# A decoder layer on one core: the mixing product in quarters of the array, and the attention's output product from rounded parts

## The reference

```python
x = x + mamba(layernorm(x), W_in, conv_w, ..., W_out)
x = x + cross_attention(layernorm(x), ctx, mask, Wq, ..., Wo, qn_w, kn_w)
x = x + bitlinear_ffn(layernorm(x), w_gate, w_up, w_down, ln_weight)
```

## Time and profile before

| | |
|---|---|
| time, median of 3 runs | 1300.21 us (1299.61 to 1300.24) |
| the profiled execution's own time | 1300.34 us |
| its span, first to last instruction | 1298.4 us |
| busy share of the span | PE 95%, weight loads 79%, DVE 79%, POOL 61%, ACT 54% |
| chain that ended last | PE 87%, DVE 5%, POOL 3% |
| mean granted clock of TensorE | 0.978 |

### The profile page before, as it was taken

How to read it: one execution, slowest core, us unless ns; L and a number is a source line. 1 busy time by engine, 2 the same in 40 slices (tenths; PEclk the granted TensorE clock), 3 DMA queues, 4 the chain that set the end, 5 groups by cost and what they waited for, 6 DMA issues and landing times.

```text
span 1298.4 us, 32119 instructions
## 1 busy us (share of the span) xinstructions
PE 1229.9 (95%) x10803; PEld 1024.4 (79%) x10803; DVE 1031.4 (79%) x2572; ACT 703.5 (54%) x1588; POOL 796.1 (61%) x1435
## 2 busy tenths in 40 slices
PE   4789999999999999999999999999999999999865
PEld 3677888888888888888888888888888888888743
DVE  3675888888888888888888888888888888888555
ACT  3564566555555655555565555556555555665432
POOL 3465666667666666766666676666667666666541
PEclk8799999999999999999999999999999999999986
DMA  8300000000000000000000000000000000000000
GB/s 272 112 13 13 10 14 18 16 12 16 16 8 12 16 16 12 16 16 8 12 16 16 12 16 16 9 11 16 16 12 16 16 12 8 12 14 13 6 5 9
DMA packets 30645, 28.62 MB, mean 22 GB/s; under 512 B 7696, under 2 KB 28944, under 8 KB 30352
## 3 DMA queue, kind: packets, MB, share of 16 engines
q1 hardware_dynamic: 27680, 28.11, 6.8%
q10 hardware_dynamic: 2928, 0.03, 0.1%
HBM read 23.93 MB, written 4.19 MB: 22 GB/s over the span
## 4 chain that ended last, share of the span: by engine, by line
PE 87%; DVE 5%; POOL 3%; issue 2%; ACT 1%; DMA 1%; POOLq 0%; DVEq 0%; SPq 0%; ACTq 0%
PE bank L1405 17%; PE bank L1315 16%; PE bank L1397 5%; PE bank L1238 5%; PE bank L1375 4%; PE bank L1288 4%; PE bank L1247 4%; PE bank L1278 3%; PE bank L1425 3%; PE bank L1210 2%; PE bank L1430 2%; PE bank L1328 2%; PE bank L1227 2%; PE bank L1443 2%; PE bank L1385 2%
## 5 line engine op out<-in xcount | busy, mean ns | idle before, releaser
L1315 PE MATMUL bank<-xcT,wq 128*128 128x128 f32 x2048 | 236.2, 276 | 1.6 <-ACT xcT L648 1.6
L1315 PEld LDWEIGHTS bank<-xcT,wq 128*128 128x128 f32 x2048 | 231.1, 192 | 6.2 <-issue 2.0
L1405 PE MATMUL bank<-wo,oT 128*128 128x256 f32 x1024 | 232.1, 380 | 0.0
L1405 PEld LDWEIGHTS bank<-wo,oT 128*128 128x128 f32 x1024 | 190.6, 191 | 23.9 <-issue 0.3
L877 DVE SCALAR_TENSOR_TENSOR xc<-bank,cw,xc 128x124 f32<-128x124 f32 (+2 forms) x576 | 163.9, 341 | 15.2 <-ACT xc L618 8.4
L663 ACT ACTIVATE qT<-bank,bqT 128x128 f32<-128x128 f32 x384 | 109.7, 369 | 47.1 <-PE bank L1315 46.8
L354 POOL TENSOR_SCALAR m_mv<-m_mv 128x1 f32<-128x1 f32 x32 | 7.7, 241 | 158.1 <-DVE m_mv L845 158.1
L422 POOL TENSOR_TENSOR rq<-rq,minus_half 128x16 f32<-128x16 f32 x32 | 93.1, 2909 | 7.8 <-DVE rq L975 7.8
L1031 DVE SCALAR_TENSOR_TENSOR h<-h,bank 128x512 f32<-128x512 f32 x64 | 44.1, 688 | 64.9 <-ACT h L702 64.9
L434 POOL TENSOR_TENSOR pr<-pr,mask 128x512 f32<-128x512 f32 x64 | 82.9, 1315 | 14.0 <-DVE pr L982 14.0
L444 POOL TENSOR_TENSOR pr<-pr,mx 128x512 f32<-128x512 f32 x64 | 65.4, 1044 | 40.3 <-DVE mx L994 40.3
(11 more groups left out here) (225 smaller groups left out, 3053.7 us busy)
## 6 DMA issues: line engine op xcount, KB each, us to landing
x_in<-in_x SPq DMA_DIRECT2D x32, 128.0 KB, 2.1
c_in<-in_ctx SPq DMA_DIRECT2D x32, 128.0 KB, 2.0
x_m<-in_x SPq DMA_DIRECT2D x32, 128.0 KB, 2.0
out<-x SPq DMA_DIRECT2D x32, 128.0 KB, 1.7
wq<-in_L_xattn_Wq SPq DMA_DIRECT2D x1, 2048.0 KB, 14.3
wo<-in_L_xattn_Wo SPq DMA_DIRECT2D x1, 2048.0 KB, 12.7
w_in<-in_L_attn_W_in SPq DMA_DIRECT2D x1, 1024.0 KB, 6.0
qT<-in_L_ffn_w_gate SPq DMA_DIRECT2D x1, 1024.0 KB, 9.4
```

The source lines that it names most:

```text
L1315: last = mm(x_Qbank[g][:, (n % 4) * P:(n % 4 + 1) * P], wq[:, c, n * HD:(n + 1) * HD], xcT[:, c, :], start=(c == 0), stop=(c == DC - 1))
L1405: last = mm(X1[:, 0:D], oT[:, n, :, :], wo[:, n, :], start=(n == 0), stop=(n == NH - 1))
```

## The change

There are two parts.

The mixing product runs in quarters. `mbd` gives way to `mw`, which holds for each sequence only its own 64 x 64 block, so DVE writes it with one operation instead of two, and the clearing goes. PE multiplies with 64 rows, 64 weight columns and 64 moving columns, 16 times (32 instructions); the first sequence's results go to M0 and the second's to M2. As M2 is also where the squares are added up, `x_sums` now waits for `m_y` and not for `m_Xdt`. The product `x * D` goes to POOL (`m_skip`, into `xd`), and DVE's gate becomes two additions in place of four operations.

The output product becomes a `split_product`. `wo` is kept as `wo_hi` and `wo_lo`, `oT` as `o_hi` and `o_lo`; that makes 48 single-pass instructions with 256 moving columns. The rounded parts come from ACT (four copies, as before). The remainders of two banks come from DVE (`x_o_low`, out of PSUM) and of the other two from POOL, out of two more ACT copies (`x_o_copy`, into `o_f`, which lies in `ksq` and `th`). ACT now adds the keys' squares up itself, with four accumulating instructions, and `x_k_sum` goes. ACT's second tanh of the feed-forward part moves ahead of the keys' squares, and DVE's `m_norm` moves behind the second `x_o_low`. The output product also waits for the remainders from X1 and F1, the key and value products wait for those steps that read their banks, and `f_up` waits for the copy out of F1. At the start Wo is loaded in two halves through one staging area; the second half is loaded when POOL has finished the first (`w_o_low`).

```diff
             def x_output(t, half):
                 if half == 0:
-                    after(pe, x_oT[1][1], t + 1)
+                    after(pe, x_ol[1][1], t + 1)
+                    after(pe, x_ol[0][1], t + 1)
                 for n in range(half * NH // 2, (half + 1) * NH // 2):
-                    last = mm(X1[:, 0:D], oT[:, n, :, :], wo[:, n, :], start=(n == 0), stop=(n == NH - 1))
+                    last = split_product(X1[:, 0:D], (o_hi[:, n, :, :], o_lo[:, n, :, :]), (wo_hi[:, n, :], wo_lo[:, n, :]),
+                                         n == 0, n == NH - 1)
...
-                for n in range(NHM):
-                    last = mm(M0[(n % 2) * HP:(n % 2 + 1) * HP, (n // 2) * P:(n // 2 + 1) * P], xdt[:, n, :], mbd[:, n, :],
-                              start=True, stop=True)
+                for j in range(XCH):
+                    for a in range(2):
+                        rows = slice(a * SEQ, (a + 1) * SEQ)
+                        for u in range(2):
+                            last = mm(m_mixed[a][u * HP:(u + 1) * HP, j * SEQ:(j + 1) * SEQ], xdt[rows, 2 * j + u, :],
+                                      mw[rows, 2 * j + u, :], start=True, stop=True)
...
+            def m_skip(t):
+                after(pool, s["m_xs"], t + 1)
+                after(pool, s["m_y"], t)
+                g.tensor_tensor(xd[:], xc[:, 0:XCH, :], bcast(d_ch[:, :].unsqueeze(2), [P, XCH, P]),
+                                ALU.mult).then_inc(s["m_xd"].sem, 1)
...
+            def x_o_low(t, n):
+                after(pool, x_of[n], t + 1)
+                heads = slice(8 * n, 8 * n + 8)
+                g.tensor_tensor(o_lo[:, heads, n, :], o_f[n], o_hi[:, heads, n, :].bitcast(F32),
+                                ALU.subtract).then_inc(x_ol[n][n].sem, 1)
+
+            def w_o_low(n):
+                pool.wait_ge(s["p_ohi"].sem, n + 1)
+                heads = slice(8 * n, 8 * n + 8)
+                g.tensor_tensor(wo_lo[:, heads, :], wo_stage, wo_hi[:, heads, :].bitcast(F32),
+                                ALU.subtract).then_inc(s["p_olo"].sem, 1)
...
-            def x_k_square(t):
+            def x_k_square(t, xb):
                 after(act, s["x_kb"], t + 1)
-                sc.activation(ksq[:], kb[:], ACT.Square).then_inc(s["x_ksq"].sem, 1)
+                if xb is not None:
+                    after(act, x_ol[0][0], xb + 1)
+                for n in range(NKV):
+                    last = sc.activation(ksq[:, n, :], kb[:, n, :], ACT.Square, accum_out=kss[:, 0, n:n + 1])
+                last.then_inc(s["x_ksq"].sem, 1)
...
-                for j in range(XCH):
-                    last = v.scalar_tensor_tensor(out=yT[:, j, :], in0=xc[:, j, :], scalar=d_ch[:, j:j + 1],
-                                                  in1=M0[:, j * P:(j + 1) * P], op0=ALU.mult, op1=ALU.add)
+                after(dve, s["m_xd"], t + 1)
+                for a in range(2):
+                    tokens = slice(a * SEQ, (a + 1) * SEQ)
+                    last = v.tensor_tensor(yT[:, :, tokens], m_mixed[a].rearrange("p (j l) -> p j l", j=XCH), xd[:, :, tokens], ALU.add)
```

More of the change, by code:

```diff
@@ L307, in _ @@
             sp.dma_start(bv_r[:], row(bv, NKV * HD)).then_inc(s["w_attn"].sem, 16)
-            sp.dma_start(wo[:], Wo.rearrange("(h p) n -> p h n", p=P)).then_inc(s["w_attn"].sem, 16)
-            for i in range(1, 5):
+            wo_rows = Wo.rearrange("(h p) n -> p h n", p=P)
+            sp.dma_start(wo_stage, wo_rows[:, 0:NH // 2, :]).then_inc(s["w_o_l"].sem, 16)
+            body(1)
+            sp.wait_ge(s["p_olo"].sem, 1)
+            sp.dma_start(wo_stage, wo_rows[:, NH // 2:, :]).then_inc(s["w_o_l"].sem, 16)
+            for i in range(2, 5):
                 body(i)
@@ L500, in body @@
                     g.tensor_tensor(wv_lo[:], wv, wv_hi[:].bitcast(F32), ALU.subtract).then_inc(s["p_lo"].sem, 1)
+                if first == 0:
+                    pool.wait_ge(s["w_skip"].sem, 16 * W_SKIP)
+                if first == 1:
+                    w_o_low(0)
+                if m is not None:
+                    m_skip(m)
+                if first == 2:
+                    w_o_low(1)
                 if f is not None:
                     f_scales(f)
+                if first == 2:
+                    pool.wait_ge(s["p_olo"].sem, 2)
+                if xb is not None:
+                    x_o_low(xb, 0)
+                    x_o_low(xb, 1)
                 if first == 0:
                     pool.wait_ge(s["w_out_l"].sem, 16)
-                    pool.wait_ge(s["w_skip"].sem, 16 * W_SKIP)
                     g.tensor_tensor(w_out[:], w_out[:], bcast(nw[:, :].unsqueeze(2), [P, XCH, D]),
@@ L725, in body @@
                     x_q_square(xa, 0)
+                if first == 1:
+                    w_o_high(0)
                 if xb is not None:
@@ L750, in body @@
                     w_sum(2)
+                if first == 2:
+                    act.wait_ge(s["q_bf"].sem, 2)
                 if xb is not None:
-                    x_o_copy(xb, 0, 0)
-                    x_o_copy(xb, 0, 1)
+                    x_o_high(xb, 0, 0)
+                    x_o_copy(xb, 0)
+                    x_o_high(xb, 1, 1)
+                    x_o_copy(xb, 1)
+                if f is not None:
+                    f_T_copy(f)
                 if xa is not None:
@@ L766, in body @@
                     m_square(m)
+                if xb is not None:
+                    x_o_high(xb, 1, 0)
                 if xa is not None or m is not None:
                     x_sums_copy(xa, m)
+                if f is not None:
+                    f_tanh(f, 1)
+                if xb is not None:
+                    x_o_high(xb, 0, 1)
                 if first == 0:
@@ L1131, in body @@
                     x_kv(xa)
-                if ms is not None and first != 0:
-                    m_norm(ms)
+                if first == 2:
+                    dve.wait_ge(s["p_olo"].sem, 2)
+                if xb is not None:
+                    x_o_low(xb, 1, 0)
                 if m is not None:
                     m_total(m)
-                if first == 0:
-                    m_norm(ms)
                 if xa is not None:
@@ L1141, in body @@
                     f_gate(f, 1)
-                if xa is not None:
-                    x_k_sum(xa)
+                if xb is not None:
+                    x_o_low(xb, 0, 1)
+                if ms is not None:
+                    m_norm(ms)
                 if first == 0:
@@ L1535, in body @@
                     m_project_z(mn)
+                if first == 2:
+                    pe.wait_ge(s["p_olo"].sem, 2)
                 if xb is not None:
```

113 lines of the change are left out of this document (61 added, 52 removed).

## The result

The changed kernel takes 1337.26 us (median of 4 runs, 1333.13 to 1338.68), the kernel before 1299.91 (1298.71 to 1300.24): 1.0284 times as long, 95% interval 1.026 to 1.0307. The forecast was 1281, in a range up to 1303. The profiled execution took 1338.68 us, of which its span is 1336.7.

What follows compares the result with a forecast made beforehand. PE's own work was taken to set the pace (busy 600.55 of 603.63 us over sixteen tiles). From 1300.34, less 23.2 for the loop, plus 3.5 at the start: 1280.6, forecast as 1281, overall range 1247 to 1303.

Steps and rivals of the forecast that it cites:

- rivals on the loads: Output product on PE: weight loads set the pace, at 0.19 each a tile is 2 us longer, 1362 us; chance 0.04.
- quarters that don't overlap: Mixing on PE: the quarter-array products don't run side by side, mixing +1.0 us, 1310 us in all; chance 0.05.
- a held `m_norm`: DVE's `m_norm`, moved back, is held by POOL's L422, each tile 0.9 us longer, 1330 us; chance 0.08.
- What POOL gets: POOL's added work, about 4 us, is hidden; `x_norm` comes 0.6 us earlier per tile, bounds 0.2 and 1.0.
- a hold for `m_xn`: DVE's normalisation step `m_norm` held beside POOL's L422, costing DVE 1.7 us between gate and residual; chance 0.08.
- rival "given back": PE's gain is lost on the way, for instance as its squares wait for the gate: 1292 to 1303 us; chance 0.13.
- the sum: Per tile 0.6 us from an earlier `x_norm` plus 0.18 ahead of the mixing: 0.8 us, 23.2 over 29 bodies.
- 1.6 and 3.4 of wait for PE: Bodies 1 and 2: POOL's remainders of Wo stall DVE's mixing multiplication and PE's mixing behind it, 1.6 and 3.4 us.
- -23.2 for the loop: The loop's 29 bodies with all stages, each 0.8 us shorter: 23.2 us gained.
- +3.5 for the start: Bodies 1 and 2: waits of 1.6 and 3.4 us, less 1.5 for the output product: 3.5 us lost.

Runs made afterwards that it cites:

- mixing only: The kernel before with only the mixing part of the change, without the new output product: 1284.01 us, 0.988 of the kernel before.
- mask behind x_xn: The changed kernel, but POOL's first mask operation also waits until DVE has written `x_xn`: 1305.83 us, 1.005 of the kernel before.
- seg_lo late too: The changed kernel with POOL's second decay multiplication (`seg_lo`) moved behind `x_split` and its first mask operation waiting for `x_xn`: 1279.89 us.
- product only, seg_lo late: The changed kernel with the mixing part undone, `seg_lo` moved behind `x_split` and POOL's mask waiting for `x_xn`: 1322.19 us.
- run 32: Not a follow-up run: "run" is a verb here, and 32 is the number of mixing products that PE does in 0.69 us.

## Why the prediction was wrong

PE's own work became shorter by about what I had, 1.6 a tile for 1.5, but by other shares: the product's two halves take 2.91 and 3.01 us, 1.2 less than before where I had 1.5, and the mixing 0.69, where I had taken 1.05 and no gain. The rivals on the loads, on quarters that don't overlap and on a held `m_norm` (L901 at 620.22, 0.40, beside L444) are refuted. POOL's additions are hidden, as forecast: no wait is left before `m_mv` (I had about 1), but 1.99 before `ssy`. They do hold DVE's gate product L995 (1.00 in place of 0.69), where DVE then has 0.99 to spare. DVE's idle time before L1065 is gone.

The step that failed is **What POOL gets**: "It can bring `x_norm` forward by its wait of 0.22 and by what it loses to DVE ... I take 0.6". Two things stand in its place. First the rows of the kernel before that I had not weighed, of DVE, and of POOL for `ssy` and the next `x_norm`:

```profile
614.45 0.41 DVE L836 TENSOR_SCALAR x_xn<-x,x_mv 128x256 f32<-128x256 f32 x1
```

```profile
635.18 0.19 POOL L404 TENSOR_SCALAR ssy<-ssy 128x1 f32<-128x1 f32 x1 [2.53 <-DVE ssy L936]
...
651.21 0.23 POOL L354 TENSOR_SCALAR x_mv<-x_mv 128x1 f32<-128x1 f32 x1 [0.22 <-DVE x_mv L832]
```

- POOL brought forward nothing. From `ssy` to `x_norm` it took 16.03 before (635.18 to 651.21), a wait of 0.22 in it, and takes 16.31 now without one. So its own way is 0.5 longer where I had taken it for up to 0.8 shorter, and even the lower bound of that term, 0.2, was too high. Each engine still holds the other up, only elsewhere: POOL's first step of the scales, of one column, now lasts until DVE's L1104 ends, 1.25 where the held one took 1.03 before (L467).

```profile
624.68 1.25 POOL L497 TENSOR_TENSOR f_sc<-f_sc 128x1 f32<-128x1 f32 x1
...
624.67 1.21 DVE L1104 TENSOR_TENSOR hh<-hh,lnw 128x1024 f32<-128x1024 f32 x1
```

- I had not asked what an earlier DVE does to the order of the next two instructions. Before, `x_xn` starts at 614.45 (the row above) and the mask at 614.61, after its wait for `pr`: a margin of 0.16. DVE comes 1.7 earlier relative to POOL now, so `pr` is ready, the mask loses its wait, and `x_xn` is held for 0.94. I had weighed a hold for `m_xn`, and it came at another place.

The way that a tile follows can be cut in three at rows of the timelines: POOL's `ssy` to its `x_norm`, from there to PE's turn of xc, and from that to the next `ssy`. Medians in us over the tiles between 400 and 1000; the sum is a tile without the low clock:

| stretch | before | mixing only | changed | mask behind x_xn | seg_lo late too | product only, seg_lo late |
|---|---|---|---|---|---|---|
| `ssy` to `x_norm` (POOL) | 16.04 | 16.04 | 16.32 | 16.34 | 15.30 | 15.33 |
| `x_norm` to the turn of xc | 11.77 | 11.78 | 12.48 | 11.97 | 11.96 | 11.96 |
| turn of xc to `ssy` | 10.00 | 9.62 | 9.61 | 9.54 | 9.53 | 10.95 |
| sum | 37.8 | 37.4 | 38.4 | 37.8 | 36.8 | 38.2 |

The output product is done on PE beside the first stretch, which POOL sets in these kernels, so what it gains doesn't shorten a tile of 37.8 or more. Only where POOL's stretch gets shorter, as with `seg_lo` late, does PE's own work become the next limit, and the product count. The mixing lies in the third, and there its 0.4 arrives. In the changed kernel that gain stands against 0.3 in the first stretch and 0.7 in the second, most of it the hold of `x_xn`; with the mask behind `x_xn` against 0.3 and 0.2, which makes nothing of it and gives the old 37.8. That comes nearest to my rival "given back", for other reasons than the squares.

From the wait of 2.25 follows another term, which the sum didn't have at all: the clock, 1.5 us in 11 tiles.

The last is the start: 8.1 and not 3.5. I had the hold of `mw` by Wo's remainders but only as 1.6 and 3.4 of wait for PE; PE's waits before the mixing are 4.10 (1.90 before) and 2.61 (none before), then 2.35 for the gate (1.29 at the squares before), and the second query product there runs partly at the low clock (9.01 in place of 7.38).

In the sum: I had -23.2 for the loop, it was +31.6 - 1.1; I had +3.5 for the start, it was +8.1.

## What to carry over

When one engine gets quicker, write down for each neighbour which of its waits vanish, and look at what follows each of them within the width of one instruction: a wait can be what keeps a holding instruction behind a short urgent one. Even work that is hidden on its own engine can hold a neighbour, as the remainder did with `f_qb`. Work taken from the busiest engine shortens a tile only where no other path runs beside it, so measure that path from its first wait to its last before counting the gain. And where PE begins to stand still in each tile, its clock can cost as much as the wait.

## What the hardware showed that I had not expected

- Products with 64 rows, 64 weight columns and 64 moving ones, spread over four quarters, run 32 in 0.69 us, 0.02 each; products with 64 moving columns over all rows took 0.033.
- Three-part products with 256 columns start 0.118 apart (48 in 5.9 us), each with its own load.
- `rq` (L444, a power on POOL, 2.91 us) doesn't hold DVE's `m_xn` (0.40), while the mask (1.27 an instruction) holds `x_xn` for 0.94, a remainder of the output product (1.27) holds `f_qb` for 1.03, and a remainder of Wo holds a multiplication of two SBUF inputs for up to 4.77.
- The granted clock falls to 0.50 after waits of PE of 2.1 to 2.3 us in a part of the tiles, also where the wait is split with 0.6 us of work between (1.39 and 0.77). In the kernels where PE waited 1.34 and 1.24 it stayed at 1.00. Throw-away work in the wait kept it at 1.00.
